# 32-head attention in a chain of four attention blocks: SyncE issues the key rows and half of the first query rows, GpSimd clears buffers before it splits weights, and TensorE runs four projections before the first norm's transposes

## The chip, the cores and the metric

The kernel runs on one core of one Trainium2 chip. The metric is the device time of one execution in microseconds (us); lower is better. The engines are TensorE (PE; its weight loads are listed as PEld), VectorE (DVE), ScalarE (ACT), GpSimd (POOL) and SyncE (SP, which only issues transfers). A transfer can be issued by SP or by POOL; each has a queue of its own, and each engine issues in its program's order.

## The reference

For each of two batch elements, 512 rows of width 512 pass through four attention blocks over a context of 1024 rows. The change touches the second block (`L1`, 32 query heads of width 16, 8 key and value heads) and the norms that follow it (its own layer norm, and at once the first layer norm of the third block):

```python
q = hidden_state @ Wq + bq
k = encoder_hidden_state @ Wk + bk
v = encoder_hidden_state @ Wv + bv
q = q.reshape(b, l, KVH, GROUPS, HD).transpose(0, 2, 3, 1, 4)   # KVH 8, GROUPS 4, HD 16
...
scores = jnp.einsum('bkgld,bksd->bkgls', q, k) * scale + mask
attn = jax.nn.softmax(scores, axis=-1)
out = jnp.einsum('bkgls,bksd->bkgld', attn, v)
out = out.transpose(0, 3, 1, 2, 4).reshape(b, l, H) @ Wo + bo
x = layer_norm(out + hidden_state) * gamma + beta
...
h = layer_norm(x, ln1_scale, ln1_offset)      # third block: 16 heads of width 128, twice, then an MLP
x = x + cross_attention(h, ctx, ...)
```

The fourth block (`latent` in the kernel) and its MLP follow. The dependence that matters: the key projection of the third block needs only the context, not the norm; its query projection needs the norm.

## The kernel before, in words

The program is a list of stages; each engine runs its own part of every stage, for batch element 0 and then for element 1. Stages are parted by a barrier of PE, ACT and DVE; SP and POOL join only some of them and run ahead otherwise. Every fp32 operand is split into a high and a low part (`fp32r`), and a product is three matmuls (`mm3`, L147 to L149).

**The stage `grouped()`** (from L535) is the 32-head attention. Its start, in order:

- SP loads the key and value weights (L624, L625), the first quarter of the query weights (L629), mask, bias row and the first quarter of the output weights (L637), then waits for splits before the next quarters.
- POOL (`pool_`) scales a bias, waits for both key and value weights, splits `wk`, the first `wq` and `wv`, clears `vd` and builds `fold` (L683 to L688, signalled as `made`), and then issues all spreads.
- PE projects keys (24 matmuls), the first quarter of the queries (12) and values (24), and turns the values. ACT and DVE take the results out as high and low parts; the semaphore `kq_done` counts the low parts of the two key halves and then of each query quarter.
- Each head needs its 16 rows three times over (keys high, low, high; queries high, high, low), and that for both halves of the partitions. `spread_k` (L639 to L644) and `spread_q` (L646 to L650) copy them there: six transfers of 16 x 512 values for each key head (8 of them) or query head (8 in a quarter).
- Then PE walks 128 steps plus a tail: step `q` makes the scores of query head `q // 4` and row tile `q % 4`, later steps transpose and multiply what DVE (L904) and ACT (L850) made of them. Step 0 waits for key head 0 and query head 0, step 4 for query heads 1 to 3, step 16 for key head 1 and query heads 4 to 7, step 32 for the other six key heads. In steps 16 to 19 PE also projects the next quarter of the queries, for which it waits on POOL's split of the second quarter of `Wq`, which waits for SP's load of it:

```python
spread_k(pool, 0, first_ready)          # after kq_done 2
spread_q(pool, 0, first_ready)          # after kq_done 3
for u in range(1, 4): spread_q(pool, u, qs_ready[0])
spread_k(pool, 1, ks_ready[0])
for u in range(4, HEADS): spread_q(pool, u, qs_ready[1])
split_q(pool, b, 1)
for kv in range(2, KV): spread_k(pool, kv, ks_ready[1])
```

**The stage `norm("n1", ..., first=...)`** follows it. DVE and ACT compute two layer norms one after the other (L1933 to L1963). PE runs `ahead_in["n1"](pe, b, 0)`, two key projections of the next stage (12 x 2 matmuls, L147 to L149 on `CT` and `w_wk`), waits for the four normalised row tiles, transposes each (L1900), and runs the other two key projections (24 matmuls). ACT and DVE scale, shift and split the transposed values (L1915 to L1972) before the barrier. The other norms are built by the same function: `n2` has the same key projections, `n3` and `n4` have none, and PE has nothing to do there between its transposes and the barrier.

**The stage `wide("1")`** begins with the query projection (12 matmuls on `XT` and `w_wq`) and the first value projection (24 matmuls 128x256), after which PE waits for DVE and ACT to take the values out.

## Time and profile before

| | us |
|---|---|
| median of 3 runs | 4287.23 |
| lowest, highest | 4285.82, 4290.34 |
| the profiled execution, its own time | 4284.18 |
| its span, first to last instruction | 4282.4 |
| PE busy | 3984.2 (93%) |
| DVE, ACT, POOL busy | 2556.9, 1868.4, 1189.7 |

The profile is of one execution. Its span leaves 1.78 us outside (4284.18 less 4282.4). Times in its rows are us from the span's start; matmuls overlap in the records, so a stretch is read from start to start. In a timeline row stand the start, the duration, the engine, the line, the operation, what it writes and reads, and in brackets the idle time before it with what ended it. Durations of matmuls tell TensorE's granted clock: at 2.4 GHz they start 0.23 us apart for 128x512, at 1.2 GHz 0.43 us.

### The profile page before, as it was taken

The numbers are of one execution on the slowest core, as the hardware profiler recorded it, in microseconds if no ns is written. First come the engines' busy times: TensorE is split into PE (matmuls) and PEld (weight loads), VectorE is DVE, ScalarE is ACT, GpSimd is POOL, SyncE is SP. The second block draws the span as 40 slices with busy tenths as digits, with TensorE's granted clock in tenths as the row PEclk, the third lists the DMA queues.
The fourth block names the chain that finished last, engine by engine and source line by source line (L and its number), as shares of the span: only waits on it lengthen the run. The fifth ranks groups of instructions, "written<-read, shape, count | busy, mean of one in ns | idle before, by whom it ended". The sixth has DMA issues, their size and how long they took to land. (4 is left out here: it accounts for less than half of the span.)

```text
span 4282.4 us, 55226 instructions
## 1 busy us (share of the span) xinstructions
PE 3984.2 (93%) x21018; PEld 2967.9 (69%) x21018; DVE 2556.9 (60%) x4134; ACT 1868.4 (44%) x3294; POOL 1189.7 (28%) x1318
## 2 busy tenths in 40 slices
PE   8899799998999989999988998999989999899988
PEld 6555588887888867543775556888878888775437
DVE  3588656556565665455636886565565656645555
ACT  3588434344443431455135884344343434314551
POOL 0642213223231323121306422132232313232213
PEclk9999899999999999999999999999999999999999
DMA  2310101011010113221403101010110101132212
GB/s 70 74 31 18 55 23 45 23 45 40 28 40 28 40 40 90 51 52 30 130 30 77 28 18 55 23 45 29 39 40 28 45 23 40 45 89 50 50 35 87
DMA packets 167573, 195.62 MB, mean 46 GB/s; under 512 B 18627, under 2 KB 123272, under 8 KB 167310
## 3 DMA queue, kind: packets, MB, share of 16 engines
q1 hardware_dynamic: 142734, 151.15, 11.6%
q0 software_dynamic: 24576, 40.94, 5.0%
q8 instruction: 169, 2.77, 0.3%
q14 instruction: 94, 0.77, 0.1%
HBM read 149.02 MB, written 2.10 MB: 35 GB/s over the span
## 5 line engine op out<-in xcount | busy, mean ns | idle before, releaser
L1337 DVE TENSOR_TENSOR w_pt_lo<-ps,w_pt_hi 128x512 fp32r<-128x512 f32 x512 | 334.7, 685 | 158.7 <-ACT w_pt_hi L1268 158.6
L1113 POOL CAST w_wo_hi<-w_raw 128x1024 fp32r<-128x1024 f32 x32 | 33.2, 1037 | 1329.7 <-PE ps L149 1324.0
L1268 ACT ACTIVATE w_pt_hi<-ps 128x512 fp32r<-128x512 f32 x512 | 281.3, 595 | 203.7 <-PE ps L1205 203.6
L904 DVE CUSTOM_DVE_ANT_0 g_units<-ps,g_mask 128x1024 f32<-128x1024 f32 x256 | 311.2, 1217 | 81.2 <-PE ps L767 81.2
L1754 ACT ACTIVATE h_pt<-ps,zero_col 128x512 f32<-128x512 f32 x384 | 257.1, 686 | 234.3 <-PE ps L1710 232.8
L1803 DVE TENSOR_REDUCE h_mxs<-ps 128x1 f32<-128x512 f32 x384 | 243.7, 684 | 162.5 <-PE ps L1699 160.8
L1320 DVE TENSOR_REDUCE w_mx<-ps 128x1 f32<-128x1024 f32 x256 | 312.0, 1219 | 33.8 <-PE ps L149 33.3
L1205 PE MATMUL ps<-ident,w_p 128*128 128x128 f32 x2048 | 279.1, 275 | 39.6 <-DVE w_pt_lo L1337 39.6
L779 PE MATMUL ps<-ident,g_units 128*128 128x128 f32 x2048 | 292.2, 284 | 19.7 <-ACT g_turned L858 17.4
L850 ACT ACTIVATE g_units<-g_units,g_nmx 128x1024 f32<-128x1024 f32 x256 | 294.6, 1151 | 18.8 <-DVE g_nmx L904 15.8
L1205 PEld LDWEIGHTS ps<-ident,w_p 128*128 128x128 f32 x2048 | 235.2, 140 | 96.2 <-DVE w_pt_lo L1337 67.1
L147 PE MATMUL ps<-w_wv_hi,CT_hi 128*128 128x256 f32 x1024 | 289.1, 282 | 8.6 <-DVE w_v_lo L1331 8.6
L779 PEld LDWEIGHTS ps<-ident,g_units 128*128 128x128 f32 x2048 | 222.0, 143 | 100.1 <-issue 64.3
L149 PE MATMUL ps<-w_wv_hi,CT_lo 128*128 128x256 f32 x1024 | 288.5, 282 | 0.0
L148 PE MATMUL ps<-w_wv_lo,CT_hi 128*128 128x256 f32 x1024 | 288.4, 282 | 0.0
L1261 ACT ACTIVATE w_p<-ps,w_nm 128x1024 f32<-128x1024 f32 x256 | 281.1, 1098 | 0.0
L1259 ACT ACTIVATE w_ex<-w_xl,w_nm 128x1 f32<-128x1 f32 x256 | 75.5, 295 | 420.7 <-DVE w_nm L1326 420.7
L1296 DVE SCALAR_TENSOR_TENSOR w_k_lo<-ps,cols,w_k_hi 128x512 fp32r<-128x512 f32 x128 | 95.7, 750 | 212.0 <-ACT w_k_hi L1243 212.0
L147 PE MATMUL ps<-w_pt_hi,w_v_hi 128*128 128x512 f32 x512 | 217.3, 424 | 0.0
L147 PE MATMUL ps<-w_k_hi,w_q_hi 128*128 128x512 f32 x512 | 210.3, 411 | 7.1 <-ACT w_p L1261 7.1
L1681 PE MATMUL ps<-h_pt,h_vd 128*64 128x512 f32 x768 | 210.5, 626 | 6.6 <-ACT h_parts L1762 6.0
L147 PEld LDWEIGHTS ps<-w_wv_hi,CT_hi 128*128 128x128 f32 x1024 | 195.9, 191 | 14.7 <-DVE w_v_lo L1331 9.4
(362 smaller groups left out, 10209.2 us busy)
## 6 DMA issues: line engine op xcount, KB each, us to landing
w_raw<-in_L_xattn_wk SPq DMA_DIRECT2D x32, 512.0 KB, 3.4
w_raw<-in_L_xattn_wq SPq DMA_DIRECT2D x32, 512.0 KB, 3.5
w_raw<-in_L_xattn_wv SPq DMA_DIRECT2D x32, 512.0 KB, 3.8
w_raw<-in_L_xattn_wo SPq DMA_DIRECT2D x32, 512.0 KB, 3.6
mlp_raw<-in_L_xattn_w_fc SPq DMA_DIRECT2D x64, 256.0 KB, 3.2
mlp_raw<-in_L_xattn_mlp_w SPq DMA_DIRECT2D x64, 256.0 KB, 3.2
h_ks<-h_k_hi POOLq DMA_DIRECT2D x64, 192.0 KB, 3.0
g_qs<-g_q_hi POOLq DMA_DIRECT2D x256, 32.0 KB, 1.9
```

Of the source, the lines that this page charges most:

```text
L147: pe.matmul(o, a[0], b[0], start=start, stop=False, skip_group_check=True)
L148: pe.matmul(o, a[0], b[1], start=False, stop=False, skip_group_check=True)
L149: return pe.matmul(o, a[1], b[0], start=False, stop=stop, skip_group_check=True)
L779: i = pe.transpose(ps[:, T_BANK + h, v * P:(v + 1) * P], units[:, k % U, (4 * h + v) * P:(4 * h + v + 1) * P], ident[:, :])
L850: act.activation(units[:, k % U, :], units[:, k % U, :], ACT.Exp, bias=nmx[:, k % U:k % U + 1], scale=-1.0, accum_out=z[:, k // 32 % 2, lt ...
L904: dve.tensor_tensor_reduce(units[:, q % U, :].rearrange("p (h w) -> p h w", h=2), ps[:, 2 * (q % 2):2 * (q % 2) + 2, :], mask[:, q % 4, :] ...
L1205: i = pe.transpose(ps[:, T_BANK + tn % 2, lt * P:(lt + 1) * P], prob[:, u, lt, v * P:(v + 1) * P], ident[:, :])
L1261: act.activation(prob[:, u, lt, :].rearrange("p (h w) -> p h w", h=2), ps[:, S_BANK + 2 * (sn % 2):S_BANK + 2 * (sn % 2) + 2, :], ACT.Exp, ...
L1268: act.activation(pt.h[:, x[2] % 4, :], ps[:, T_BANK + tn % 2, :], ACT.Copy).then_inc(t_hi, 1)
L1320: dve.tensor_reduce(mx[:, u, lt:lt + 1], ps[:, S_BANK + 2 * (sn % 2):S_BANK + 2 * (sn % 2) + 2, :], AX.XY, ALU.max).then_inc(max_own, 1)
L1337: dve.tensor_tensor(pt.l[:, x[2] % 4, :], ps[:, T_BANK + tn % 2, :], as_f32(pt.h[:, x[2] % 4, :]), ALU.subtract).then_inc(t_free, 1)
L1754: act.activation(pt[:, j, :], ps[:, T_BANK_ + (m * KT + j) % 2, :], ACT.Exp, bias=zero_col[:, :], scale=SCALE).then_inc(e_done, 1)
```

## The change

Three things:

1. In `grouped()`, SP issues all spreads of keys, and those of query heads 4 to 7 of the first quarter, under three semaphores (`first_key`, `ks_ready`, `later_rows`); POOL keeps the query heads 0 to 3 and all spreads of later quarters. On SP they stand after the load of the first quarter of `Wo` and ahead of the load of the second quarter of `Wq`: 12 transfers of keys, 24 of queries, 36 of keys, 72 in all for each batch element. SP reads them as fp32, since both sides are 4-byte values.
2. POOL clears `vd` and builds `fold` before it waits for the key and value weights, not after the splits.
3. In the norm `n1`, PE runs all four key projections ahead of the transposes.

```diff
@@ -574,6 +574,7 @@
             loaded = {k: sem(f"{tag}_loaded_{k}") for k in ("kv", "q", "o", "b", "m")}
             split = {k: sem(f"{tag}_split_{k}") for k in ("kv", "q", "o")}
             made, first_ready = sem(tag + "_constants_made"), sem(tag + "_first_ready")
+            first_key, later_rows = sem(tag + "_first_key"), sem(tag + "_later_rows")
             pre_full, kq_hi, kq_done, v_done = (sem(tag + x) for x in ("_pre_full", "_kq_hi", "_kq_done", "_v_done"))
             ks_ready, qs_ready = ([sem(f"{tag}_{n}_ready{i}") for i in range(2)] for n in ("ks", "qs"))
             s_full, s_free = sem(tag + "_scores_full"), sem(tag + "_scores_free")
@@ -619,6 +620,19 @@
 
             def ring_wait(eng, b, x):
                 eng.wait_ge(ring_full, b * n_ring + ring_at[x] + 1)
+
+            def spread_k(eng, kv, ready):
+                for h in range(2):
+                    for blk, src in enumerate((kd.h, kd.l, kd.h)):
+                        at_ = 64 * h + DH * blk
+                        eng.dma_start(as_f32(ks[at_:at_ + DH, kv, :]),
+                                       as_f32(src[kv * DH:(kv + 1) * DH, h * 512:(h + 1) * 512])).then_inc(ready, 16)
+
+            def spread_q(eng, u, ready):
+                for h in range(2):
+                    for blk, src in enumerate((qd.h, qd.h, qd.l)):
+                        at_ = 64 * h + DH * blk
+                        eng.dma_start(as_f32(qs[at_:at_ + DH, u, :]), as_f32(src[u * DH:(u + 1) * DH, :])).then_inc(ready, 16)
 
             def sp_(sp, b):
                 sp.dma_start(raw_k[:, :, :], w_k.rearrange("(k p) n -> p k n", p=P)).then_inc(loaded["kv"], 16)
@@ -635,19 +649,15 @@
                                      ).then_inc(loaded["b"], 16)
                     upto(sp, split["o"], g)
                     sp.dma_start(raw_o[:, :], w_o.rearrange("(c p) n -> c p n", p=P)[c, :, :]).then_inc(loaded["o"], 16)
-
-            def spread_k(pool, kv, ready):
-                for h in range(2):
-                    for blk, src in enumerate((kd.h, kd.l, kd.h)):
-                        at_ = 64 * h + DH * blk
-                        pool.dma_start(ks[at_:at_ + DH, kv, :],
-                                       src[kv * DH:(kv + 1) * DH, h * 512:(h + 1) * 512]).then_inc(ready, 16)
-
-            def spread_q(pool, u, ready):
-                for h in range(2):
-                    for blk, src in enumerate((qd.h, qd.h, qd.l)):
-                        at_ = 64 * h + DH * blk
-                        pool.dma_start(qs[at_:at_ + DH, u, :], src[u * DH:(u + 1) * DH, :]).then_inc(ready, 16)
+                    if c == 0:
+                        sp.wait_ge(kq_done, b * KQ + 2)
+                        spread_k(sp, 0, first_key)
+                        sp.wait_ge(kq_done, b * KQ + 3)
+                        spread_k(sp, 1, ks_ready[0])
+                        for u in range(4, HEADS):
+                            spread_q(sp, u, later_rows)
+                        for kv in range(2, KV):
+                            spread_k(sp, kv, ks_ready[1])
 
             def spread_rz(pool, n):
                 pool.wait_ge(rz_done, n)
@@ -676,28 +686,21 @@
 
             def pool_(pool, b):
                 pool.tensor_scalar(bq_s[:, :], cols[:, c_bq:c_bq + C], 0.25, None, ALU.mult)
-                pool.wait_ge(loaded["kv"], b * 32 + 32)
-                split_kv(pool, wk, raw_k)
-                split_q(pool, b, 0)
-                split_kv(pool, wv, raw_v)
                 pool.memset(vd[:, :, :, :], 0.0)
                 pool.memset(fold[:, :], 0.0)
                 for j in range(4):
                     pool.drain()
                     pool.tensor_tensor(fold[:, :], fold[:, :], ident[:, 32 * j:32 * j + 32], ALU.add)
                 pool.drain().then_inc(made, 1)
-                pool.wait_ge(kq_done, b * KQ + 2)
-                spread_k(pool, 0, first_ready)
+                pool.wait_ge(loaded["kv"], b * 32 + 32)
+                split_kv(pool, wk, raw_k)
+                split_q(pool, b, 0)
+                split_kv(pool, wv, raw_v)
                 pool.wait_ge(kq_done, b * KQ + 3)
                 spread_q(pool, 0, first_ready)
                 for u in range(1, 4):
                     spread_q(pool, u, qs_ready[0])
-                spread_k(pool, 1, ks_ready[0])
-                for u in range(4, HEADS):
-                    spread_q(pool, u, qs_ready[1])
                 split_q(pool, b, 1)
-                for kv in range(2, KV):
-                    spread_k(pool, kv, ks_ready[1])
                 split_o(pool, b, 0)
                 for c in range(1, C):
                     g = b * C + c
@@ -750,13 +753,17 @@
                     if q < STEPS:
                         n, i_, u = b * STEPS + q, q % 4, q % 32 // 4
                         if q == 0:
-                            pe.wait_ge(first_ready, (b + 1) * 2 * 6 * 16)
+                            pe.wait_ge(first_ready, (b + 1) * 6 * 16)
+                            pe.wait_ge(first_key, (b + 1) * 6 * 16)
                         elif q == 4:
                             pe.wait_ge(qs_ready[0], (b * 15 + 3) * 6 * 16)
                         elif q % 32 == 0:
                             pe.wait_ge(qs_ready[0], (b * 15 + 3 + 4 * c) * 6 * 16)
                         elif q % 32 == 16:
-                            pe.wait_ge(qs_ready[1], (b * C + c + 1) * 4 * 6 * 16)
+                            if c:
+                                pe.wait_ge(qs_ready[1], (b * (C - 1) + c) * 4 * 6 * 16)
+                            else:
+                                pe.wait_ge(later_rows, (b + 1) * 4 * 6 * 16)
                         if q == 16:
                             pe.wait_ge(ks_ready[0], (b + 1) * 6 * 16)
                         elif q == 32:
@@ -1894,13 +1901,15 @@
             def pe_(pe, b):
                 if tag in ahead_in:
                     ahead_in[tag](pe, b, 0)
+                    if first:
+                        ahead_in[tag](pe, b, 1)
                 for lt in range(LT):
                     pe.wait_ge(xn_done, run(b) * LT + lt + 1)
                     for c in range(KC):
                         i = pe.transpose(ps[:, S_BANK + c, lt * P:(lt + 1) * P], xn[:, lt, c * P:(c + 1) * P], ident[:, :])
                         if lt == LT - 1:
                             i.then_inc(turned, 1)
-                if tag in ahead_in:
+                if tag in ahead_in and not first:
                     ahead_in[tag](pe, b, 1)
                 barrier(pe, done, b)
 
```

The first place is POOL from the start of `grouped()` on, in batch element 0. `g_wk`, `g_wq` and `g_wv` are the split weights, `g_raw_` the loaded ones, `g_vd` and `g_fold` the cleared buffers, `g_ks` and `g_qs` the spread keys and queries. Before:

```order
L659 CAST g_wk_hi<-g_raw_k 128x512
L661 TENSOR_TENSOR g_wk_lo<-g_raw_k,g_wk_hi 128x512
L671 TENSOR_SCALAR g_raw_q<-g_raw_q 128x512
L673 CAST g_wq_hi<-g_raw_q 128x512
L675 TENSOR_TENSOR g_wq_lo<-g_raw_q,g_wq_hi 128x512
L659 CAST g_wv_hi<-g_raw_v 128x512
L661 TENSOR_TENSOR g_wv_lo<-g_raw_v,g_wv_hi 128x512
L683 MEMSET g_vd 128x3072
L684 MEMSET g_fold 128x32
L687 TENSOR_TENSOR g_fold<-g_fold,ident 128x32 x4
L643 DMA g_ks<-g_k_hi 16x512
L643 DMA g_ks<-g_k_lo 16x512
```

And of the changed kernel:

```order
L689 MEMSET g_vd 128x3072
L690 MEMSET g_fold 128x32
L693 TENSOR_TENSOR g_fold<-g_fold,ident 128x32 x4
L669 CAST g_wk_hi<-g_raw_k 128x512
L671 TENSOR_TENSOR g_wk_lo<-g_raw_k,g_wk_hi 128x512
L681 TENSOR_SCALAR g_raw_q<-g_raw_q 128x512
L683 CAST g_wq_hi<-g_raw_q 128x512
L685 TENSOR_TENSOR g_wq_lo<-g_raw_q,g_wq_hi 128x512
L669 CAST g_wv_hi<-g_raw_v 128x512
L671 TENSOR_TENSOR g_wv_lo<-g_raw_v,g_wv_hi 128x512
L635 DMA g_qs<-g_q_hi 16x512 x2
L635 DMA g_qs<-g_q_lo 16x512
```

The clears moved from between the splits and the spreads to ahead of the splits, and POOL's first spread is now one of queries.

The second place is SP in the same stage, from the loads of the first quarters on. Before:

```order
L634 DMA g_bo<-in_L_xattn_bo 128x512
L637 DMA g_raw_o<-in_L_xattn_Wo 128x512
L629 DMA g_raw_q<-in_L_xattn_Wq 128x4x128
L637 DMA g_raw_o<-in_L_xattn_Wo 128x512
L629 DMA g_raw_q<-in_L_xattn_Wq 128x4x128
```

Of the changed kernel, the first spreads, and then the last ones:

```order
L648 DMA g_bo<-in_L_xattn_bo 128x512
L651 DMA g_raw_o<-in_L_xattn_Wo 128x512
L628 DMA g_ks<-g_k_hi 16x512
L628 DMA g_ks<-g_k_lo 16x512
L628 DMA g_ks<-g_k_hi 16x512 x2
L628 DMA g_ks<-g_k_lo 16x512
```

```order
L628 DMA g_ks<-g_k_hi 16x512 x2
L628 DMA g_ks<-g_k_lo 16x512
L628 DMA g_ks<-g_k_hi 16x512
L643 DMA g_raw_q<-in_L_xattn_Wq 128x4x128
L651 DMA g_raw_o<-in_L_xattn_Wo 128x512
```

The load of the second quarter of `Wq`, which came next after the first `Wo` load, now stands behind 72 spreads.

The third place is PE in the norm `n1` of batch element 0, around its transposes (`n_xn` is the normalised input, `w_wk` and `w_wq` the next stage's key and query weights). Before:

```order
L147 MATMUL ps<-CT_hi,w_wk_hi 128x512
L148 MATMUL ps<-CT_lo,w_wk_hi 128x512
L149 MATMUL ps<-CT_hi,w_wk_lo 128x512
L1900 MATMUL ps<-ident,n_xn 128x128 x16
L147 MATMUL ps<-CT_hi,w_wk_hi 128x512
L148 MATMUL ps<-CT_lo,w_wk_hi 128x512
L149 MATMUL ps<-CT_hi,w_wk_lo 128x512
```

And of the changed kernel:

```order
L147 MATMUL ps<-CT_hi,w_wk_hi 128x512
L148 MATMUL ps<-CT_lo,w_wk_hi 128x512
L149 MATMUL ps<-CT_hi,w_wk_lo 128x512
L1909 MATMUL ps<-ident,n_xn 128x128 x16
L147 MATMUL ps<-XT_hi,w_wq_hi 128x512
L148 MATMUL ps<-XT_lo,w_wq_hi 128x512
L149 MATMUL ps<-XT_hi,w_wq_lo 128x512
```

Before, 24 matmuls of the key projections stood on either side of the transposes; now 48 stand ahead of them, and behind them comes the next stage's query projection.

## Rows read from the trace of the kernel before

**Rows 1.** The page: busy us, share of the span and instructions of each engine.

```profile
PE 3984.2 (93%) x21018; PEld 2967.9 (69%) x21018; DVE 2556.9 (60%) x4134; ACT 1868.4 (44%) x3294; POOL 1189.7 (28%) x1318
```

**Rows 2.** Timeline of PE, first steps of `grouped()`: start, us, line, operation, [idle before <-releaser].

```profile
162.05 0.80 PE L767 MATMUL ps<-g_ks,g_qs 48*128 48x512 f32 x2 [3.12 <-DMA g_qs<-g_q_lo]
...
2299.38 0.79 PE L767 MATMUL ps<-g_ks,g_qs 48*128 48x512 f32 x2 [2.92 <-DMA g_qs<-g_q_lo]
```

**Rows 3.** Timeline of POOL, start of `grouped()`, both batch elements.

```profile
132.67 0.61 POOL L659 CAST g_wk_hi<-g_raw_k 128x512 fp32r<-128x512 f32 x1 [3.47 <-DMA g_raw_v<-in_L_xattn_Wv]
...
140.25 2.67 POOL L683 MEMSET g_vd<- 128x3072 f32 x1
...
145.20 0.74 POOL L643 DMA_DIRECT2D g_ks<-g_k_hi  x1 [0.64 <-issue]
...
146.41 1.37 POOL L643 DMA_DIRECT2D g_ks<-g_k_hi  x2
...
148.97 0.96 POOL L650 DMA_DIRECT2D g_qs<-g_q_hi  x2
...
2270.07 0.61 POOL L659 CAST g_wk_hi<-g_raw_k 128x512 fp32r<-128x512 f32 x1 [4.36 <-DMA g_raw_v<-in_L_xattn_Wv]
...
2286.24 0.97 POOL L650 DMA_DIRECT2D g_qs<-g_q_hi  x2
```

**Rows 4.** Timeline of DVE, the mask pass that follows the first query part.

```profile
146.40 2.49 DVE L893 TENSOR_SCALAR g_mask<-g_mask 128x1024 f32<-128x1024 f32 x4
...
2283.67 2.49 DVE L893 TENSOR_SCALAR g_mask<-g_mask 128x1024 f32<-128x1024 f32 x4
```

**Rows 5.** Timeline of SP's queue: issues of small, of wide, and of a long transfer.

```profile
24.12 0.42 SPq L2169 DMA_DIRECT2D vec<-in_L_xattn_bias_v  x1
...
129.83 0.50 SPq L629 DMA_DIRECT2D g_raw_q<-in_L_xattn_Wq  x1
...
2267.43 0.99 SPq L634 DMA_DIRECT2D g_bo<-in_L_xattn_bo  x1
```

**Rows 6.** Tile `g_raw_q`: splits, then landing, of the `Wq` quarters; ns min/median/max.

```profile
L671 POOL TENSOR_SCALAR g_raw_q<-g_raw_q x8: 1492/1908/2032, 134.7 to 2455.9; 128x512 f32<-128x512 f32 x8
...
L675 POOL TENSOR_TENSOR g_wq_lo<-g_raw_q,g_wq_hi x8: 1275/1288/1293, 137.1 to 2462.7; 128x512 fp32r<-128x512 f32 x8
...
DMA to landing us min/median/max: 3.1/4.0/4.7
```

**Rows 7.** Timeline of PE at step 16: first matmul of the next query quarter.

```profile
189.37 0.50 PE L147 MATMUL ps<-XT_hi,g_wq_hi 128*128 128x512 f32 x1
```

**Rows 8.** Timeline of PE, norm `n1` and start of `wide("1")`, both batch elements.

```profile
477.67 3.68 PE L1900 MATMUL ps<-ident,n_xn 128*128 128x128 f32 x16 [7.40 <-DVE n_xn L1963]
...
488.22 0.47 PE L147 MATMUL ps<-XT_hi,w_wq_hi 128*128 128x512 f32 x1 [0.26 <-PEq L232]
...
496.11 0.38 PE L147 MATMUL ps<-w_wv_hi,CT_hi 128*128 128x256 f32 x1 [2.14 <-DVE w_v_lo L1331]
...
2616.64 3.67 PE L1900 MATMUL ps<-ident,n_xn 128*128 128x128 f32 x16 [7.41 <-DVE n_xn L1963]
...
2626.16 0.47 PE L147 MATMUL ps<-XT_hi,w_wq_hi 128*128 128x512 f32 x1 [0.26 <-PEq L232]
```

**Rows 9.** Timeline of PE in norms `n4`, `n3` and `n2` and in what follows.

```profile
1029.94 1.91 PE L1900 MATMUL ps<-ident,n_xn 128*128 128x128 f32 x16
...
2051.71 0.76 PE L147 MATMUL ps<-XT_hi,mlp_w_hi 128*128 128x512 f32 x1 [5.00 <-DVEq L232]
...
2060.20 0.47 PE L147 MATMUL ps<-mlp_w_hi,mlp_g_hi 128*128 128x512 f32 x1 [0.23 <-DVE mlp_g_lo L2101]
...
3715.38 3.80 PE L1900 MATMUL ps<-ident,n_xn 128*128 128x128 f32 x16 [6.16 <-DVE n_xn L1963]
...
3723.48 0.76 PE L147 MATMUL ps<-XT_hi,mlp_w_hi 128*128 128x512 f32 x1 [4.30 <-DVEq L232]
...
3730.80 0.47 PE L147 MATMUL ps<-mlp_w_hi,mlp_g_hi 128*128 128x512 f32 x1 [0.29 <-DVE mlp_g_lo L2101]
```

## The prediction

> **What bounds the kernel now.** I read the page's engine line first: PE is busy 93% of the span [rows 1], so a gain must come out of PE's idle or half-clock stretches, and each counts in full, since everything later hangs on PE. The timeline of PE through the two places that the change touches shows which stretches these are.
>
> The first is the start of `grouped()`. PE waits for landed queries twice in each batch element: ahead of step 0 and ahead of step 4, there for 3.12 and 2.92 us [rows 2]. The second wait decides, because the few steps that step 0 lets through are done by then. What is late is POOL's queue of spreads, issued 0.48 us apart (six take 2.86 us). POOL issues key head 0 first (145.20 to 148.97) and query head 0 only then, at 148.97 [rows 3], though DVE had the query part ready when its mask pass began, at 146.4 [rows 4]. In element 1 the same two times are 2286.24 and 2283.67 [rows 3, 4].
>
> The second is norm `n1`. PE does its first two key projections, idles 7.40 us, and does its transposes at the 1.2 GHz level (3.68 us for 16). The other 24 key matmuls follow, and the next stage's query projection begins at 488.22, 0.26 us after them: PE ends this stage, not DVE [rows 8]. From the start of the transposes to that projection pass 10.55 us in element 0 and 9.52 in element 1 [rows 8].
>
> **The change part by part.**
>
> *Clears ahead of the splits (POOL).* They last from 140.25 to 144.56 (145.20 less the 0.64 of idle), 4.3 us [rows 3]. POOL idles ahead of its first split for 3.47 us in element 0 and 4.36 in element 1, waiting for a load [rows 3]. So the clears delay the splits, and with them keys, queries and values, by 4.3 - 3.47 = +0.85 us in element 0 and by nothing in element 1. If the load were earlier, the cover would go and up to 4.3 us would show.
>
> *Key head 0 on SP.* POOL can start query head 0 as soon as that is ready: in element 0 at 146.4 + 0.85 = 147.3 and not 148.97, a gain of 1.7 us; in element 1 at 2283.7 and not 2286.24, 2.5 us. But this puts POOL's first spreads under DVE's mask pass of 2.49 us. There POOL's transfers cost more: two took 1.37 us, 0.69 each, against 0.48 [rows 3, 4]. About four fall in it, some 0.15 more each, so 0.6 us goes back. Step 4 comes 1.1 us earlier in element 0 and 1.9 in element 1. SP's transfers now land at the same time as POOL's; the trace has no such pair. Below, the price is nothing; above, I put one further issue slot, 0.5 us, on the last landing. I take 0.15 for each element. Sum of the stage: 1.1 + 1.9 - 0.3 = **2.7 us gained**. With the full slowing (0.5 each, 0.69 for five transfers) it is 1.5, without any 4.2.
>
> *The other spreads on SP.* Query heads 4 to 7 and key head 1 are due at step 16, the rest at step 32; from POOL they came in time. New is that the second quarter of `Wq` is loaded behind 72 issues. The nearest row is a small transfer of 16 rows on SP, 0.42 us, some 0.46 from one to the next; a wide load costs 0.50, or 0.55 with its gap [rows 5]. SP's first six issues start when the keys are ready, 12 matmuls of 0.23 us ahead of the queries' 147.3, and end at about 147.7; 66 more at 0.46 end at 178.0. With 0.4 for its own issue, 4.0 to land, and POOL's split (1.91 + 0.61 + 1.29) [rows 3, 6], the split is done at 186.2. PE wants it at 189.37 less the 1 us gained, 188.4 [rows 7]: 2.2 us of slack, so I cost it at **nothing**. At 0.55 an issue it is 3.8 us late, and PE stands in front of everything queued behind: scores, transposes, products. POOL loses 72 issues of 0.48, 34 us for each element, but is no bound there. Nothing else waits on SP before that.
>
> *Four key projections ahead of the transposes.* The 24 moved matmuls at 2.4 GHz (0.23 us apart) take 5.5 of the 7.40 us of idle, so nothing of them delays the transposes. What ends the stage then is the chain over ACT and DVE. Its length shows in `n3`, which has nothing behind its transposes: from 3715.38 to the next stage's matmul at 3723.48, 8.10 us, with transposes at 1.2 GHz as here [rows 9]. Gain: 10.55 - 8.10 = 2.45 and 9.52 - 8.10 = 1.42. If the transposes run at 2.4 GHz, as in `n2` (1.91 us for 16) [rows 9], the chain begins about 1.35 us earlier; with 1.9 us of idle ahead of them instead of 7.40 I give that one chance in two, +0.7 each.
>
> Against it stands the clock behind the chain. PE now idles 4 to 5 us between transposes and query projection. After idle of 4.30 us in `n3`, 24 matmuls took 3723.48 to 3730.80, less a wait of 0.29: 7.03 us; after 5.00 us in `n4`, 2051.71 to 2060.20, less 0.23: 8.26 [rows 9]. At 2.4 GHz they take 5.5. The query and first value projection here are as much work, and the latency behind them (PE next starts at 496.11) hides none of it [rows 8]. So 1.5 to 2.7 us come back as half-clock time; I take 2.1. Sum over both elements: 2.45 + 1.42 + 1.4 - 4.2 = **1.0 us gained**, between -1.5 (slow transposes, 2.7 twice) and +3.6 (fast transposes, 1.5 twice).
>
> The Trainium skill, "TensorE: Matmul & The Clock Gate", Part 1, says that the half rate is the array's default and that only sustained activity releases it; by this rule alone the move gains nothing beyond idle time turned into slow time, and the sum would be the 2.7 us of the other stage.
>
> Together 2.7 + 1.0 = 3.7 us. The profiled execution took 4284.18, so 4280.5 like for like; it lies 3.05 us under the median of the runs, 4287.23, and against that I forecast **4283.5 us**.
>
> **The rivals.** A measurement of this kernel can tell about 0.2%, 8.6 us, from no change; nothing in the sum is that large.
>
> - *Both clocks fall well.* Transposes at 2.4 GHz, a short slow tail behind them, no slowing under the mask pass, and step 4 early enough that PE is not at half clock for steps 4 to 6 (step 4's two scores took 0.80 us [rows 2]). Then 3.6 + 4.2 + about 2 = 9.8 us: 4277.5. For it: the transposes of `n2`. Against: all three slow rows behind idle.
> - *The norm's move gives nothing.* The slow tail is the long one and the transposes stay slow: -1.5 with 2.7 or 1.5: 4286 to 4287.5. For it: `n4`'s long tail, and every row here that follows idle of 4 us or more is slow. The clock rule named above is this rival's.
> - *SP at 0.55 an issue.* The split is up to 3.8 us late in each element: 3.7 - 7.6, so 4291 at worst.
> - *SP becomes the bound (slower).* The place is PE's wait at step 16. The split is late from about 0.50 us an issue on, and each further 0.01 us costs 0.66 us an element. The gain is eaten at 0.53, and 8.6 us are lost from 0.59 on. A row for SP at 0.99 us exists [rows 5], a 128-row transfer. No row shows SP copying between partitions. At 0.65: 2 x 66 x 0.15 = 19.8 lost, 3.7 won: 4303.
>
> That the change doesn't do what it says is excluded by the order shown: the instructions stand where it puts them.
>
> **How the numbers follow.** Forecast (4280 to 4286): 0.50. Clocks fall well (4277.5): 0.17. Norm gives nothing (up to 4287.5): 0.16. SP at about 0.55 (up to 4291): 0.07. SP the bound (4303): 0.10. Faster by over 0.2% needs less than 4278.6: the second case and the forecast's best end, 0.18. Slower by over 0.2%: 0.10. Within: 0.72. The range 4277 to 4291 takes in the first four cases, with the bounds of the unknown costs, and leaves out the last and the edge of the second.
>
> **What would show it.** In `grouped()`: POOL's first spread at about 147.4 and 2283.8, PE's step 4 1 and 2 us earlier, SP's spreads at 0.46 us, and no PE wait on a split of `Wq` at step 16. In the norm: 24 more matmuls ahead of the transposes with 2 us of idle left, the next stage's first matmul 6.7 to 8.1 us after the transposes begin, and its projections half of the time at 1.2 GHz. SP issues over 0.5 us would make the first part wrong; a query projection at 2.4 GHz throughout, or an ACT and DVE chain longer than in `n3`, the second.

## The result, and the profile after

The kernel with the change took **4299.18 us** (median of 7 runs, 4297.76 to 4304.81), the kernel before in the same session 4286.19 (4283.12 to 4290.34). The ratio is 1.0032, with a 95% interval of 1.0021 to 1.0044: 13 us slower, outside the forecast's range of 4277 to 4291 and on its other side. The profiled execution took 4300.41 us, its span 4298.6.

The page's engine line, beside [rows 1]:

```profile
PE 3980.5 (93%) x21018; PEld 2967.9 (69%) x21018; DVE 2557.7 (60%) x4134; ACT 1868.3 (43%) x3294; POOL 1119.0 (26%) x1174
```

PE did the same work and was busy 3.7 us less, in a span that is 16.2 us longer: it stood idle for 19.9 us more. The view to read is therefore the waits of PE, here from 130 to 240 us (start of `grouped()`, element 0), largest first:

```profile
PE ps L147 <- POOL g_wq_lo L685: 11.3, 1, 11.3
PE ps L147 <- POOL g_wk_lo L671: 4.9, 1, 4.9
PE ps L774 <- DMA g_qs<-g_q_lo: 2.9, 1, 2.9
```

The first line is new: one wait of 11.3 us for the low part of a `Wq` quarter. The timeline of PE shows where, in both batch elements; the rows answer to [rows 2, 7]:

```profile
163.13 0.80 PE L774 MATMUL ps<-g_ks,g_qs 48*128 48x512 f32 x2 [2.92 <-DMA g_qs<-g_q_lo]
...
202.29 0.80 PE L147 MATMUL ps<-XT_hi,g_wq_hi 128*128 128x512 f32 x1 [11.27 <-POOL g_wq_lo L685]
...
2306.86 0.80 PE L774 MATMUL ps<-g_ks,g_qs 48*128 48x512 f32 x2 [2.71 <-DMA g_qs<-g_q_lo]
...
2345.19 0.80 PE L147 MATMUL ps<-XT_hi,g_wq_hi 128*128 128x512 f32 x1 [10.35 <-POOL g_wq_lo L685]
```

This is the first matmul of the second query quarter, the wait at step 16. What it waits for, on POOL's queue in the same execution:

```profile
149.09 1.60 POOL L635 DMA_DIRECT2D g_qs<-g_q_hi  x2 [6.81 <-DVE g_q_lo L888]
...
196.62 1.48 POOL L681 TENSOR_SCALAR g_raw_q<-g_raw_q 128x512 f32<-128x512 f32 x1 [35.34 <-DMA g_raw_q<-in_L_xattn_Wq]
200.22 0.61 POOL L683 CAST g_wq_hi<-g_raw_q 128x512 fp32r<-128x512 f32 x1 [2.12 <-issue]
200.98 1.26 POOL L685 TENSOR_TENSOR g_wq_lo<-g_raw_q,g_wq_hi 128x512 fp32r<-128x512 f32 x1
```

POOL, free of 72 issues, stands idle for 35.34 us until the quarter lands. From there to the end of the split pass 5.6 us, 2.12 of them idle between scaling and cast (more on this in the last section). And SP's queue, which loads the quarter:

```profile
146.07 0.62 SPq L628 DMA_DIRECT2D g_ks<-g_k_hi  x1
146.73 0.58 SPq L628 DMA_DIRECT2D g_ks<-g_k_lo  x1
147.36 1.22 SPq L628 DMA_DIRECT2D g_ks<-g_k_hi  x2
148.62 0.59 SPq L628 DMA_DIRECT2D g_ks<-g_k_lo  x1
...
192.84 0.59 SPq L628 DMA_DIRECT2D g_ks<-g_k_hi  x1
193.48 0.58 SPq L643 DMA_DIRECT2D g_raw_q<-in_L_xattn_Wq  x1
```

One spread costs SP 0.59 us and follows the last after 0.63 to 0.64; 72 of them with a few longer ones fill 146.07 to 193.48, 47.4 us. The forecast had 0.46 each and the last at 178.0. In element 1 the load leaves at 2336.57. SP kept this pace after POOL had issued its last spread, at 161.3, so it is no contention with POOL's queue.

The norm, answering to [rows 8]:

```profile
492.49 3.48 PE L1909 MATMUL ps<-ident,n_xn 128*128 128x128 f32 x16 [1.92 <-DVE n_xn L1972]
500.25 0.76 PE L147 MATMUL ps<-XT_hi,w_wq_hi 128*128 128x512 f32 x1 [4.28 <-DVEq L232]
511.04 0.38 PE L147 MATMUL ps<-w_wv_hi,CT_hi 128*128 128x256 f32 x1 [2.15 <-DVE w_v_lo L1338]
...
2634.82 2.03 PE L1909 MATMUL ps<-ident,n_xn 128*128 128x128 f32 x16 [1.92 <-DVE n_xn L1972]
2641.45 0.77 PE L147 MATMUL ps<-XT_hi,w_wq_hi 128*128 128x512 f32 x1 [4.60 <-DVEq L232]
```

The idle time ahead of the transposes fell from 7.40 to 1.92 us; from transposes to query projection pass 7.76 and 6.63 us (before 10.55 and 9.52), and that projection starts at half clock (0.76 for its first matmul, before 0.47).

Where the 16.2 us lie in these two traces, by the stages as they are cut in the table further below: the attention stage took 13.5 and 10.3 us more, the norm 2.7 and 3.9 less; the first stage began 1.0 later, the stretch between the two elements was 2.8 shorter and the end 0.7 longer.

**Theory 1:** the loss is the `Wq` quarter behind SP's 72 issues, two waits of 21.6 us together; the norm's edit and the rest gain. **Theory 2:** the loss lies in the norm's order or in the spreads' transfers, and the wait at step 16 would only move elsewhere.

### The profile page after: what moved, and what is told of

It is laid out like the page before. It is cut to its first block and busy times, and to the rows that moved or that the text cites. A ratio compares the mean times of both kernels' runs of the same rounds, so it can differ in the third digit from the quotient of the medians.

```text
span 4298.6 us, 55227 instructions
## 1 busy us (share of the span) xinstructions
PE 3980.5 (93%) x21018; PEld 2967.9 (69%) x21018; DVE 2557.7 (60%) x4134; ACT 1868.3 (43%) x3294; POOL 1119.0 (26%) x1174
## 5 line engine op out<-in xcount | busy, mean ns | idle before, releaser
L1327 DVE TENSOR_REDUCE w_mx<-ps 128x1 f32<-128x1024 f32 x256 | 311.9, 1218 | 32.5 <-PE ps L149 32.3
L147 PE MATMUL ps<-CT_hi,w_wk_hi 128*128 128x512 f32 x512 | 200.8, 392 | 3.9 <-DVEq L232 3.9
```

The source lines that it names most:

```text
L147: pe.matmul(o, a[0], b[0], start=start, stop=False, skip_group_check=True)
L1327: dve.tensor_reduce(mx[:, u, lt:lt + 1], ps[:, S_BANK + 2 * (sn % 2):S_BANK + 2 * (sn % 2) + 2, :], AX.XY, ALU.max).then_inc(max_own, 1)
```

## The experiments

Each kernel's time is the median of 5 to 11 executions, that of the probe of the issues a single one. Ratios are against the kernel before on the same chip, with 95% intervals; its median there was 4282.12 to 4284.24 us, so the ratios say more than the times do.

### The load ahead of the spreads: `e1_load_first`

```diff
                     if c == 0:
+                        upto(sp, split["q"], g + 1)
+                        sp.dma_start(raw_q[:, :, :], w_q.rearrange(...)[1, :, :, :]).then_inc(loaded["q"], 16)
                         sp.wait_ge(kq_done, b * KQ + 2)
                         spread_k(sp, 0, first_key)
```

(and no such load at `c == 1`)

> The change, with the second quarter of Wq's load issued by SyncE ahead of its spreads instead of behind all 72 of them. Theory 1 (SyncE's queue: 72 issues 0.63 us apart hold the load back until 193.48 and 2336.57, and PE waits 11.27 and 10.35 us for its split ahead of the second q projection): both waits are gone, and the time is 4299.2 - 21.6 = 4277.6, between 4275 and 4281; PE shows no wait over 1 us for g_wq_lo in either stage. Theory 2 (the loss comes from the norm's order and the clock behind it, or from the transfers' contention, and the wait would merely move to the next resource, the key rows on SyncE at step 32): the time stays above 4290.

Measured: 4271.45 us, ratio 0.9975 (0.9964 to 0.9986). The load leaves at 140.14. The waits of PE from 130 to 240 us in this kernel, largest first:

```profile
PE ps L147 <- POOL g_wk_lo L675: 4.9, 1, 4.9
PE ps L778 <- DMA g_qs<-g_q_lo: 2.9, 1, 2.9
PE ps L790 <- ACT g_turned L869: 2.2, 7, 0.5
```

No wait for `g_wq_lo` is left, in either element, and none takes its place. Theory 1 holds: by ratios the change lost 0.32% and this kernel gains 0.25%, so one moved load is worth 0.57%, 24 us (some 18 to 31 by the two intervals). The times alone can't tell this from the 21.6 of the two waits, but the traces can: the attention stage of the change was 13.1 and 12.4 us longer than here, 25.5 together. The windows of both kernels show what came on top of the waits: stretch, its length, busy time of PE, PEld, DVE, ACT, POOL, then PE's granted clock. In the change:

```profile
190.00:202.00 12.00, 1.03 (x9) 0.12 (x8) 0.83 (x3) 1.56 (x3) 3.11 (x3) 0.74 0.16 41
202.00:208.00 6.00, 5.71 (x24) 3.29 (x24) 1.92 (x3) 1.72 (x3) 2.07 (x3) 0.66 0.31 87
```

With the load ahead:

```profile
190.00:202.00 12.00, 12.00 (x78) 6.56 (x70) 7.99 (x14) 7.91 (x14) 0.84 (x2) 1.00 0.22 62
202.00:208.00 6.00, 5.76 (x40) 3.25 (x38) 5.56 (x10) 5.54 (x10) 6.00 (x14) 1.00 0.37 69
```

Behind the wait PE runs for some 4 us at the 1.2 GHz level (granted 0.66 in that stretch) and gets 24 matmuls done where the other gets 40. Four us at half clock are about 2 us lost, and 11.3 + 2 is near the 13.1. The wait costs its own length and the half-clock stretch behind it.

### The load behind 60 spreads: `e5_load_after60`

```diff
                         for kv in range(2, KV):
+                            if kv == KV - 2:
+                                upto(sp, split["q"], g + 1)
+                                sp.dma_start(raw_q[:, :, :], ...[1, :, :, :]).then_inc(loaded["q"], 16)
                             spread_k(sp, kv, ks_ready[1])
```

> The change, with the second quarter of Wq's load issued by SyncE behind 60 of its 72 spreads (between key heads 5 and 6), neither ahead of all nor behind all. Theory 1 (the time of PE's wait is the time of that issue): the load leaves 12 x 0.64 = 7.7 us earlier than in the change, the waits of 11.27 and 10.35 us shrink to 3.6 and 2.7, and the time is 15.4 below the change's: 4299.2 - 15.4 = 4283.8, 12 us above the kernel with the load ahead. Theory 2 (any long run of issues on SyncE's queue costs, wherever the load stands): as the change. Theory 3 (the load's place matters little once some spreads stand behind it): as the load ahead, 4271 to 4274.

Measured: 4280.84 us, ratio 0.9991 (0.9982 to 1.0000), between the change and the load ahead. By ratios it lies 18 us under the change, where 15.4 was expected. The timeline of PE at step 16:

```profile
192.77 0.50 PE L147 MATMUL ps<-XT_hi,g_wq_hi 128*128 128x512 f32 x1 [3.43 <-POOL g_wq_lo L690]
...
193.67 0.80 PE L779 MATMUL ps<-g_ks,g_qs 48*128 48x512 f32 x2
...
2325.39 0.51 PE L147 MATMUL ps<-XT_hi,g_wq_hi 128*128 128x512 f32 x1 [2.74 <-POOL g_wq_lo L690]
```

3.43 and 2.74 us, where 3.6 and 2.7 were expected. The wait follows the place of the load by SP's issue time; theories 2 and 3 are out. A short wait has its half-clock stretch as well, only a little later: the first three matmuls behind it are fast, the fourth is slow, and in the windows of this kernel PE's clock is then at its lower level:

```profile
193.00:195.00 2.00, 2.00 (x8) 1.15 (x8) 0.49 (x1) 0.00 (x0) 1.55 (x2) 0.68 0.07 16
195.00:197.00 2.00, 2.00 (x11) 1.17 (x13) 1.27 (x3) 1.39 (x2) 0.00 (x0) 0.50 0.54 147
197.00:199.00 2.00, 2.00 (x13) 0.67 (x5) 0.16 (x1) 0.34 (x2) 0.00 (x0) 0.97 0.38 115
```

The attention stage was 4.4 us longer than in `e1_load_first` in each element, for waits of 3.43 and 2.74 us.

### What an issue on SP costs: `e6_issue_probe`

```diff
+                    if c == 1:
+                        sp.wait_ge(kq_done, b * KQ + 3)
+                        for at_, rows, n_ in ((0, 16, 512), (16, 4, 512), (32, 16, 128), (64, 64, 512)):
+                            for r in range(2, KV):
+                                sp.dma_start(as_f32(ks[at_:at_ + rows, r, 0:n_]), as_f32(kd.h[0:rows, 0:n_])).then_inc(probed, 16)
+                        sp.wait_ge(s_free, b * STEPS + 2)
+                        for r in range(6):
+                            sp.dma_start(brow[16 * r:16 * r + 16, :], t["L1_xattn_bo"].unsqueeze(0).broadcast_to([DH, D])).then_inc(probed, 16)
```

(SP, kernel before; `brow` gets its own values again; POOL waits for all of them ahead of key heads 2 to 7)

> The kernel before with 30 further issues on SyncE's queue behind the second Wq load, where it stood idle, six of each of five forms: from SBUF to SBUF 16 rows of 2 KB (the spreads' form), 4 rows of 2 KB, 16 rows of 512 B, 64 rows of 2 KB; and from DRAM to SBUF 16 rows of 2 KB. GpSimd waits for them ahead of key heads 2 to 7, long after they have landed. The outputs are the reference's, since all of it is overwritten or holds the same values. It measures why the change's issues cost 0.59 each (0.63 apart) where small loads from DRAM cost 0.42 in the kernel before. Theory A (the source decides): all four SBUF forms 0.59 or nearly so, the DRAM form 0.42 to 0.50. Theory B (the rows decide): the 4-row form is near 0.45, 64 rows over 0.8, and 16 rows from DRAM 0.59 as well. Theory C (the bytes decide): 16 rows of 512 B like the 4-row form, well under 16 rows of 2 KB. The time stays within 2 us of before.

Measured: one time, 4294.31 us. The issues of element 0, six of a form: minimum, median and maximum in ns, starts of the first and the last. In order: 16 rows of 2 KB, 4 rows of 2 KB, 16 rows of 512 B, 64 rows of 2 KB, and from DRAM 16 rows of 2 KB.

```profile
L641 SPq DMA_DIRECT2D g_ks<-g_k_hi x6: 585/590/620, 146.3 to 149.5; - x6
...
L641 SPq DMA_DIRECT2D g_ks<-g_k_hi x6: 577/601/826, 150.1 to 153.6; - x6
...
L641 SPq DMA_DIRECT2D g_ks<-g_k_hi x6: 536/590/604, 154.2 to 157.3; - x6
...
L641 SPq DMA_DIRECT2D g_ks<-g_k_hi x6: 592/765/1388, 157.9 to 162.1; - x6
...
L645 SPq DMA_DIRECT2D g_bo<-in_L_xattn_bo x6: 310/520/1173, 163.5 to 167.4; - x6
```

Four times fewer rows or four times fewer bytes save nothing: theories B and C are out for these sizes. The 64-row form starts from the same price (0.592 at the least); its median is higher by the long issues among its six. An issue whose source is SBUF took at least 0.536 us, one from DRAM at least 0.310. That leans to theory A, but the DRAM form stood right behind the 64-row one, with long issues among its six and 0.78 from start to start, so its own price was not measured cleanly. Against a simple price by source speaks the load of a `Wq` quarter from DRAM: it took 0.38 us where SP had stood idle (`e1_load_first`, 140.14), 0.50 right behind another load (130.66 there) and 0.58 right behind the spreads (193.48 in the change), while the first spread after an idle SP took 0.62. Theory A stays a leaning. For the forecast the first line is what counts: this form costs 0.59 on SP, 0.64 from start to start, with nothing else changed.

The one time is 10 us over the median of before, where at most 2 were expected: from the stage's first load to the norm's first weight load passed 318.1 and 319.9 us, before 314.7 and 316.8, 3 us more each. In element 0 PE waited 2.96 us ahead of step 0 and 3.54 ahead of step 4, before 1.35 and 3.12, and the granted clock from 163 to 200 us was 0.87, before 0.96: thirty further issues and their transfers do reach the spreads that PE waits for. They moved 1.28 MB, 0.79 of it in the 64-row form, so the 0.15 us that the forecast took for contention is neither confirmed nor refuted by this.

### The parts alone: `e2_norm_only`, `e3_no_norm`, `e4_key0_only`, `e7_clears_only`

The first is the kernel before with

```diff
                     ahead_in[tag](pe, b, 0)
+                    if first:
+                        ahead_in[tag](pe, b, 1)
...
-                if tag in ahead_in:
+                if tag in ahead_in and not first:
```

> The kernel before with only the norm's edit: four projections ahead of the first norm's transposes. Theory 1: a small gain. From the transposes' start to v.1 the changed kernel lost 0.11 in element 0 and gained 0.56 in element 1, and v.1 then ran at 2.4 GHz where before its matmuls began at 1.2 GHz (3.65 against 5.24 us to the scores), so 1 to 2 us more per element: 4286.2 - (1 to 4) = 4282 to 4285. Theory 2: this edit is what costs: 4296 to 4300.

The second is the change without these lines.

> The change without the norm's edit. Theory 1: the waits of some 11 and 10 us ahead of the second q projection are there as in the change, and the norm's small gain is missing: 4299.2 + (1 to 4) = 4300 to 4303. Theory 2: the loss is gone with the norm's edit: 4284 to 4289.

Measured: norm alone 4278.80, ratio 0.9991 (0.9982 to 1.0000); the change without it 4302.81, ratio 1.0046 (1.0034 to 1.0059), with the waits at step 16 still there (10.90 and 9.47 us). Both go the way of theory 1: the loss is there without the norm's edit and not with it alone, so theory 2's norm is out. That the edit gains is not yet clear of noise in these two.

The third is the kernel before with the clears first and

```diff
+                        sp.wait_ge(kq_done, b * KQ + 2)
+                        spread_k(sp, 0, first_key)
...
-                spread_k(pool, 0, first_ready)
```

> The kernel before with the clears ahead of the splits and only key head 0's six rows on SyncE; all other spreads stay on GpSimd in the order of before, no norm's edit. SyncE then issues 6 spreads (3.8 us at 0.63) ahead of the second Wq load, far from the 72 that make PE wait. Theory 1: no wait at the second q projection; the start of the stage gives 0 to 2 us per element (step 4 lay 33.26 and 32.44 us behind the stage's first issue, before 33.20 and 34.01): 4282 to 4286. If instead this part costs, because GpSimd's clears delay the first split, it is 4287 to 4290.

The fourth moves only the clears (memsets and the fold tile's build).

> The kernel before with the clears and the fold tile's build moved ahead of GpSimd's splits, and nothing else. The prediction priced this alone at +0.85 in element 0 and 0 in element 1, since the spreads would still wait for the key's and query's copies: 4286.2 + 0.9. If what GpSimd does between its splits and its spreads held the start back in before (3.47 and 4.36 us idle were there), nothing is gained; if the clears' 4.3 us stood on the path, it is faster by up to 2 us per element.

Measured: 4280.92, ratio 0.9993 (0.9985 to 1.0002), and 4281.49, ratio 0.9994 (0.9985 to 1.0003). Neither can be told from no change. In the trace of the clears alone step 0 comes 25.01 and 24.63 us behind the issue of the stage's first load, in that of before 24.41 and 25.42: 0.6 later in element 0, where 0.85 was forecast, and 0.8 earlier in element 1, where nothing was.

### Are the other 66 spreads worth moving: `e8_key0_norm`

`e4_key0_only` with the norm's edit.

> The kernel before with the clears first, key head 0 alone on SyncE, and the norm's edit: what the kernel with the load ahead has, less the 66 other spreads on SyncE. If parts add up and the other 66 give nothing (both q projection and step 32 are reached without a wait either way), it equals the kernel with the load ahead: 0.9975 of before, 4276; from the single parts -3.9 for the norm and -3.0 for the clears with key head 0, so -7, 4279. If moving the 66 gives something by itself (a faster GpSimd, less idle at steps 4 and 16), it is slower than the kernel with the load ahead by over 3 us.

Measured: 4270.70, ratio 0.9971 (0.9959 to 0.9982), not to be told from the load ahead (0.9975). The 66 further spreads on SP give nothing that the timings show: POOL was busy for 1118.1 us there and for 1180.6 here, and the 62.5 us bought no time.

### The norm's edit in place: `e9_load_first_no_norm`

> The change with the Wq load ahead of SyncE's spreads, without the norm's edit; against the kernel with the load ahead it gives the price of the norm's edit alone. Theory C (the edit gives the clock back: with four projections in the wait for the normalised rows the stretch 24 to 34 us behind the first weight load ran at a granted clock of 1.00 against 0.70 to 0.87 without, and from that load to the third wk load the stage took 82.8 and 82.5 us on average over five kernels with the edit, 85.6 and 85.6 over five without): slower than with it by 2.8 + 3.1 = 5.9, 4271.5 + 5.9 = 4277.4, between 4274 and 4280. Theory P (what the prediction said, the time won ahead of the transposes is given back behind them): 1.0 slower, 4272.5.

Measured: 4282.30, ratio 0.9997 (0.9988 to 1.0006), against 0.9975 with the edit: 0.22%, 9 us (some 3 to 16 by the two intervals). Theory P's 1.0 us is out; theory C's 5.9 lies inside. `e8_key0_norm` against `e4_key0_only` also gives 0.22%, norm alone 0.09%, the change against the one without it 0.14%; these last two are not clear of noise.

The windows of norm `n1`, element 1, at the same distances behind the first weight load (24 to 34, 34 to 44, 44 to 52 and 52 to 60 us). Without the edit (this kernel):

```profile
2605.10:2615.10 10.00, 3.02 (x14) 2.13 (x12) 9.27 (x25) 0.41 (x2) 0.00 (x0) 0.86 0.00 0
2615.10:2625.10 10.00, 9.32 (x41) 8.02 (x42) 5.91 (x12) 3.99 (x7) 0.00 (x0) 0.80 0.00 0
2625.10:2633.10 8.00, 5.85 (x37) 5.15 (x38) 4.35 (x11) 2.96 (x5) 5.84 (x4) 0.98 0.20 66
2633.10:2641.10 8.00, 8.00 (x44) 7.19 (x44) 3.09 (x5) 1.88 (x2) 5.99 (x5) 0.80 0.39 101
```

With it (`e1_load_first`):

```profile
2595.90:2605.90 10.00, 8.27 (x37) 6.45 (x35) 9.27 (x22) 0.41 (x2) 0.00 (x0) 1.00 0.00 0
2605.90:2615.90 10.00, 5.22 (x24) 4.23 (x25) 7.62 (x17) 5.08 (x8) 1.13 (x2) 0.81 0.04 14
2615.90:2623.90 8.00, 5.85 (x34) 5.17 (x33) 2.66 (x4) 1.86 (x3) 7.24 (x5) 0.81 0.14 48
2623.90:2631.90 8.00, 6.21 (x43) 5.36 (x41) 4.23 (x8) 3.07 (x4) 3.42 (x2) 1.00 0.58 166
```

In the first stretch PE fills the wait with 37 instead of 14 matmuls, at full clock, and the transposes then run fast. The third row is the give-back: with the edit PE is at 0.81 there, behind its idle. In the fourth it is at 1.00, and without the edit at 0.80.

One element of one pair is not enough for this: in element 0 of the same two kernels the fourth stretch reads the other way (0.85 with the edit, 1.00 without), and there the stage gained 1.0 us only. The mean granted clocks of all kernels of the table below, element 0 / element 1, by the distance behind the same load:

| stretch, us | with the edit (six) | without (five) |
| --- | --- | --- |
| 24 to 34 | 1.00 / 1.00 | 0.79 / 0.80 |
| 34 to 44 | 0.78 / 0.76 | 0.76 / 0.75 |
| 44 to 52 | 0.87 / 0.87 | 1.00 / 0.99 |
| 52 to 60 | 0.95 / 1.00 | 0.87 / 0.79 |
| 60 to 72 | 1.00 / 0.91 | 0.93 / 0.86 |

The edit loses clock in the third row and has more of it in the two below. From 44 to 84 us the clock missing from full speed adds up to 1.4 and 2.2 us with it, 2.4 and 3.4 without. So on balance, and on average, the edit gives nothing back behind the transposes, and single stages differ from this either way.

### One head more on SP: `e10_row3_too`

```diff
                         spread_k(sp, 0, first_key)
+                        sp.wait_ge(kq_done, b * KQ + 3)
+                        spread_q(sp, 3, third)
...
-                for u in range(1, 4):
+                for u in range(1, 3):
```

(on `e8_key0_norm`, with step 4 waiting for `third` as well)

> The kernel with clears first, key head 0 on SyncE and the norm's edit, and one more head: query head 3's six spreads also on SyncE, behind key head 0's, so that GpSimd issues 18 instead of 24 ahead of step 4. There PE waited 2.2 to 2.9 us for g_qs. If that wait is GpSimd's queue (6 x 0.49 = 2.9 us), it falls to under 0.5 us in both stages: 2 x 2.2 less, 4270.7 - 4.4 = 4266.3. If it is the softmax chain's or the landing's, the wait is replaced and the time stays within 1.5 us of 4270.7. SyncE's queue then holds 12 issues (7.7 us) ahead of the second Wq load, and no wait for it may appear.

Measured: **4268.80 us**, ratio 0.9966 (0.9952 to 0.9979), the lowest of all, though not to be told from `e8_key0_norm` by the intervals. The waits of PE from 130 to 240 us:

```profile
PE ps L147 <- POOL g_wk_lo L668: 4.9, 1, 4.9
PE ps L789 <- ACT g_turned L868: 2.3, 8, 0.5
PE ps L777 <- DVE g_nmx L914: 1.7, 2, 1.1
```

The wait for `g_qs` at step 4 is gone in both elements, so it was POOL's queue: six issues fewer ahead of it. By its trace the stage took 310.8 and 311.9 us against 314.0 and 314.7.

### The stages of all traces side by side

One execution each; "attention" runs from the issue of `g_raw_k`'s load to the first `wk` load of norm `n1`, "norm" from that load to the second `wk` load after it (us, element 0 / element 1).

| kernel | attention | norm |
| --- | --- | --- |
| before | 314.7 / 316.8 | 86.5 / 85.2 |
| the change | 328.2 / 327.1 | 83.9 / 81.4 |
| e1_load_first | 315.1 / 314.7 | 83.0 / 83.4 |
| e2_norm_only | 315.4 / 316.9 | 82.8 / 81.5 |
| e3_no_norm | 327.9 / 326.6 | 83.8 / 85.0 |
| e4_key0_only | 314.2 / 316.7 | 87.0 / 85.8 |
| e5_load_after60 | 319.5 / 319.1 | 81.6 / 82.7 |
| e7_clears_only | 315.4 / 315.0 | 84.0 / 86.1 |
| e8_key0_norm | 314.0 / 314.7 | 82.7 / 83.4 |
| e9_load_first_no_norm | 315.2 / 318.0 | 84.0 / 85.2 |
| e10_row3_too | 310.8 / 311.9 | 81.0 / 83.1 |

The two rows with the load behind all 72 spreads stand out in the attention, by 12.5 us or more in element 0 and 8.6 or more in element 1; the others, except the one behind 60, took 310.8 to 315.4 and 311.9 to 318.0. One trace is good to 1 to 3 us here: `e1_load_first` and `e9_load_first_no_norm` have the same attention stage and differ by 3.3 in element 1. In the norm the six with the edit average 82.5 / 82.6, the five others 85.1 / 85.5.

## Why the prediction was wrong, point by point

- **The issue on SP, the step that failed.** "The nearest row is a small transfer of 16 rows on SP, 0.42 us, some 0.46 from one to the next" took a load from DRAM for the price of a copy inside SBUF, and the upper bound of 0.55 was another load from DRAM. It measured 0.59, 0.63 to 0.64 from start to start, and 0.66 on average over the 72. The mechanism was in the text: "late from about 0.50 us an issue on, and each further 0.01 us costs 0.66 us an element". At 0.66 that gives 0.16 x 66 = 10.6 us an element; PE waited 11.27 and 10.35. The rival "SP becomes the bound" was right in the place, and with 0.65 near the 0.66 of an issue; it got 1 chance in 10. That its time came so near (4303 foretold, 4299 measured) is in part luck: it left out the half-clock stretch behind each wait and had the gains at 3.7, and both were too small. The text itself had the warning: "No row shows SP copying between partitions." The range should have reached to a case that decides at 0.59 when the only rows stop at 0.55 and one stands at 0.99.
- **The slack.** 2.2 us of slack behind a sum of 72 equal terms is 0.03 us a term. "I cost it at **nothing**" was a choice that no row supported to that precision. The last terms of the sum were off as well: landing took 3.1 us and not 0.4 + 4.0, the split 5.6 and not 1.91 + 0.61 + 1.29, which adds the lengths of three instructions and leaves out POOL's idle between them. Together 8.8 instead of 8.2, so 0.6 of the 2.2 us were not there at any price of an issue.
- **The price of a late split.** It was counted as its own length. The half-clock stretch behind it came on top: the attention stage was longer by 13.1 and 12.4 us against `e1_load_first`, for waits of 11.27 and 10.35. With the load behind 60 spreads it was longer by 4.4 each, for 3.43 and 2.74.
- **Key head 0 on SP and the clears, 2.7 us gained.** With both in place and no wait (`e1_load_first`, `e4_key0_only`, `e8_key0_norm`, `e9_load_first_no_norm`) the attention stage averages 314.6 and 316.0, without them (before, `e2_norm_only`) 315.0 and 316.8: 1.2 us together, less than what one trace is good to. Right in sign, half the size, and no timing here can tell it from nothing. Step 4, foretold 1.1 and 1.9 us earlier, came 0.1 later in element 0 (33.26 us behind the stage's first load, before 33.20) and 1.6 earlier in element 1 (32.44, before 34.01). POOL's first spread came at 149.09 and not at the foretold 147.4: the stage began 1.0 us later in this execution, and the clears, priced at 0.85, delayed DVE's low query part by 1.3 (18.2 us behind the first load, before 16.9). The sum's lower bound is also wrong by its own terms: with 0.5 for each element and 0.21 more for five transfers in each, 4.2 - 1.0 - 2.1 is 1.1 and not 1.5.
- **The norm's move, 1.0 us gained.** Its steps held: idle 1.92 us left, transposes fast in one element of two (2.03 and 3.48 us), 6.63 and 7.76 us to the query projection, and from there to the next wait's end 10.79 us in element 0 against 7.89 before, a give-back of 2.9 us. That is more than the 1.5 to 2.7 that the sum allowed, and by these steps the move would gain nothing in element 0. What failed is where the account ended. It stopped at that wait and left out that PE's clock beyond it changes too: from 52 to 60 us 0.95 and 1.00 with the edit against 0.87 and 0.79 without, on average. The stage gained 2.6 and 2.9 us by the averages of the traces, and the pairs of timings say 4 to 9 us in all, the two of 9 clear of noise.
- **The clock rule.** The Trainium skill, "TensorE: Matmul & The Clock Gate", Part 1, has the throttled state as the default and activity as what releases it. The traces agree: behind the wait of 11.27 us the granted clock was 0.66, and 1.00 once PE had worked again. The prediction drew from it a sum in which the move gains nothing, and that conclusion was wrong: with work in the idle stretch the clock was 1.00 there instead of 0.79 and 0.80, and on average higher from 52 us on.
- **The sum.** Two waits with their half-clock stretches, 25.5 us lost, less 5.5 from the norm and 1.2 from the start, is 18.8; measured 13.0, with 9.0 to 18.9 by the ratio's interval. The parts read from single traces reach the upper end of it. What is left over was not settled: the stretch from the norm's end to the next attention stage, which no edit touches, took between 1729.3 and 1737.3 us in these traces.

## What to carry to other kernels

When work moves to a queue that "has nothing to do", look for what is queued behind it: here one load, worth 24 us, stood behind 72 issues, and putting it ahead turned a kernel 0.32% slower into one 0.25% faster. Price an issue by a row of the same engine and the same kind of transfer; where none exists and the number is multiplied by 72, measure it or let the range hold the case in which it is wrong. Take the length of a chain of instructions from its first start to its last end, not from their lengths added up. And fill a wait of PE with work that is due soon anyway: here the gain did not end with the wait, because the clock behind it changed as well.

## What the hardware showed that was not expected

- The same transfer (16 rows of 2 KB, SBUF to SBUF) costs SP 0.59 us to issue (0.63 to 0.64 from start to start) and POOL 0.484. Moving issues from GpSimd to SyncE made each dearer. Why is open.
- The price on SP did not fall with rows (4 instead of 16: 0.60) or bytes (512 B instead of 2 KB a row: 0.59), and 64 rows began at the same 0.59.
- Issues cost POOL a second time, later. Between the scaling of the second `Wq` quarter and its cast stands a `drain()`, and POOL is idle there with no releaser named: 2.12 us in the change, though it had issued nothing for 35 us, and 5.05 before:

```profile
181.29 0.61 POOL L673 CAST g_wq_hi<-g_raw_q 128x512 fp32r<-128x512 f32 x1 [5.05 <-issue]
```

  The idle goes by the number of transfers that POOL issued since its last `drain()`: 2.12 us behind 24, 3.10 behind 36, 4.07 behind 48, 4.56 behind 54, 5.05 behind 60, and some 0.15 behind none (the change, before, `e8_key0_norm` and `e10_row3_too`). That is 0.082 us for each, so one issue costs POOL 0.57 us in all, still under SP's 0.63. What the engine does in that time no run shows.
